# Two diagonal tiles of a head in one bank, masked by a product on the tensor engine

## The reference

```python
q, k, v = jnp.split(jnp.clip(qkv, -8, 8), 3, axis=-1)
q, k = _layer_norm(q, q_ln_w, q_ln_b), _layer_norm(k, k_ln_w, k_ln_b)
...
scores = jnp.einsum('bqhd,bkhd->bhqk', q, k) * HEAD_DIM ** (-0.5)
rel = pos[None, :] - pos[:, None]
bias = slopes[:, None, None] * rel.astype(jnp.float32)
scores = jnp.where(rel <= 0, scores + bias[None], -jnp.inf)
probs = jax.nn.softmax(scores, axis=-1)
attn = jnp.einsum('bhqk,bkhd->bqhd', probs, v)
```

## Time and profile before

| | us |
|---|---|
| median of 3 runs | 1939.48 (1938.72 to 1940.89) |
| the profiled execution | 1937.06 |
| its span, first to last instruction | 1935.3 |
| PE busy | 1842.5 (95%) |
| DVE busy | 1137.5 (59%) |
| POOL busy | 986.4 (51%) |
| ACT busy | 475.4 (25%) |
| pieces on PE, L1823, 384 products | 136.5 |
| masked maxima on DVE, L1698, 256 entries | 115.0 |
| unmasked maxima on DVE, L1702, 128 | 83.2 |

### The profile page before, as it was taken

One profiled execution on the slowest core, in us unless ns is written; L12 is line 12 of the kernel. 1 busy time (PEld: TensorE's weight loads), 2 busy tenths in 40 slices (PEclk: granted clock), 3 DMA queues, 4 the chain that ended last, 5 costly groups with the idle time before them and its releaser, 6 DMA issues. The chain is left out here.

```text
span 1935.3 us, 27511 instructions
## 1 busy us (share of the span) xinstructions
PE 1842.5 (95%) x10157; PEld 1445.1 (75%) x10157; DVE 1137.5 (59%) x1939; ACT 475.4 (25%) x623; POOL 986.4 (51%) x1148
## 2 busy tenths in 40 slices
PE   6999999999999999999999789998889999988998
PEld 5888888888888888888888568886654444357887
DVE  6674674874856747748747733304676888535601
ACT  4221111221211212112112120002414666633200
POOL 5676755755846657557535455444711121235432
PEclk9999999999999999999999899998987999899999
DMA  2111111111111111111101122202043333011112
GB/s 95 46 55 57 45 42 46 43 50 40 43 41 46 49 41 43 39 42 49 49 14 54 44 67 82 68 22 73 3 80 52 56 54 54 2 34 46 48 49 71
DMA packets 50501, 93.57 MB, mean 48 GB/s; under 512 B 8752, under 2 KB 13488, under 8 KB 50032
## 3 DMA queue, kind: packets, MB, share of 16 engines
q1 hardware_dynamic: 49776, 91.13, 17.3%
q10 hardware_dynamic: 640, 1.31, 0.4%
HBM read 76.15 MB, written 2.10 MB: 40 GB/s over the span
## 5 line engine op out<-in xcount | busy, mean ns | idle before, releaser
L366 POOL TENSOR_TENSOR a_w_l<-a_raw,a_w_h 128x1024 fp32r<-128x1024 f32 x96 | 205.6, 2141 | 8.0
L711 DVE TENSOR_TENSOR x<-x,a_ps 128x1024 f32<-128x1024 f32 x64 | 78.0, 1219 | 167.9 <-PE a_ps L165 167.9
L1596 ACT ACTIVATE a_pr<-a_ps 128x1024 f32<-128x1024 f32 (+1 forms) x192 | 153.3, 812 | 90.2 <-PE a_ps L1803 73.2
L1546 POOL TENSOR_SCALAR_AFFINE_SELECT a_pr<-a_pr 128x256 f32<-128x256 f32 x128 | 52.0, 406 | 217.0 <-ACT a_pr L1596 215.3
L1823 PE MATMUL a_ps<-a_K,a_Q 64*128 64x512 f32 (+2 forms) x384 | 136.5, 448 | 11.5 <-DVE a_mx L1702 8.8
L165 PE MATMUL a_ps<-a_tt_h,a_w_l 128*128 128x512 f32 x376 | 147.1, 391 | 0.0
L164 PE MATMUL a_ps<-a_tt_l,a_w_h 128*128 128x512 f32 x376 | 146.6, 390 | 0.0
L163 PE MATMUL a_ps<-a_tt_h,a_w_h 128*128 128x512 f32 x376 | 146.5, 390 | 0.0
L72 POOL TENSOR_TENSOR tick<-neg_half 128x1 f32<-128x1 f32 x120 | 35.0, 292 | 215.2 <-PE a_ps L165 208.1
L1698 DVE CUSTOM_DVE_ANT_0 a_masked<-a_ps,a_mask 128x384 bf16<-128x384 f32 (+3 forms) x256 | 115.0, 486 | 32.5 <-PE a_ps L1823 31.2
L1823 PEld LDWEIGHTS a_ps<-a_K,a_Q 64*128 64x128 f32 x384 | 66.7, 198 | 84.7 <-DVE a_mx L1702 33.4
(11 more groups left out here) (247 smaller groups left out, 4727.7 us busy)
## 6 DMA issues: line engine op xcount, KB each, us to landing
a_raw<-in_a_wpair SPq DMA_DIRECT2D x96, 256.0 KB, 2.7
f_raw<-in_f_w SPq DMA_DIRECT2D x33, 320.0 KB, 2.9
a_raw_s<-in_a_wout SPq DMA_DIRECT2D x32, 256.0 KB, 3.2
f_raw<-in_f_w SPq DMA_DIRECT2D x32, 256.0 KB, 2.6
a_raw_s<-in_a_wv SPq DMA_DIRECT2D x28, 256.0 KB, 2.6
a_cst<-in_a_cst SPq DMA_DIRECT2D x32, 129.0 KB
a_Q<-a_q_h SPq DMA_DIRECT2D x64, 64.0 KB
a_K<-a_k_h SPq DMA_DIRECT2D x54, 64.0 KB
```

What stands on the lines that cost most here:

```text
L366: nc.gpsimd.tensor_tensor(to_l, src, to_h, ALU.subtract).then_inc(s(done), 1)
L711: nc.vector.tensor_tensor(a, a, units[i], ALU.add).then_inc(s("out_added"), 1)
L1546: nc.gpsimd.affine_select(tri, tri, [[0, 2], [1, P]], ALU.is_ge, 0.0, base=0, channel_multiplier=-1).then_inc(s("selected"), 1)
L1596: nc.scalar.activation(pr[n % SLOTS][:, 2 * i:2 * i + 2, 0:width], S[at % 2][:, :, skip:skip + width], ACT.Exp, scale=0.25).then_inc(s("sc ...
```

## The change

The pieces of width 128 of tiles 0 and 4, and those of width 256 of tiles 1 and 5, are made as one item: two score products of 256 columns into the two halves of a bank, each followed by a product `laterb` x `identb` that adds a large negative number above the diagonal of its last 128 columns. One TENSOR_REDUCE takes both maxima. A pair has 20 items and not 24. `AHEAD` and the two bounds around outputs and rows are moved to the same places in the new list, `V_AT` spreads the eight parts over 20 pieces, `paced` counts both tiles of an item, and ACT makes `identb` and `laterb` before it issues its loads.

```diff
--- before.py
+++ after.py
@@ -1290,13 +1290,13 @@
 STEPS += [(kt, max(BANK, kt * P), T - max(BANK, kt * P)) for kt in range(NT)]
 NS = len(STEPS)
 
-PIECES = [(4, 0, BANK, False), (0, 0, P, True), (5, 0, BANK, False), (4, 1, P, True),
-          (6, 0, BANK, False), (1, 0, 2 * P, True), (7, 0, BANK, False), (5, 1, 2 * P, True),
-          (3, 0, BANK, True), (2, 0, 3 * P, True), (7, 1, BANK, True), (6, 1, 3 * P, True)]
+PIECES = [(((4, 0),), BANK, False), (((0, 0), (4, 1)), P, True), (((5, 0),), BANK, False),
+          (((6, 0),), BANK, False), (((1, 0), (5, 1)), 2 * P, True), (((7, 0),), BANK, False),
+          (((3, 0),), BANK, True), (((2, 0),), 3 * P, True), (((7, 1),), BANK, True), (((6, 1),), 3 * P, True)]
 PIECES = [(h, *piece) for piece in PIECES for h in range(2)]
 NP = len(PIECES)
-AHEAD = 8
-V_AT = {2 + 3 * i: (AFTER + i // KT, i % KT) for i in range(2 * KT)}
+AHEAD, MIDDLE, BEHIND = 6, 12, 6
+V_AT = {2 + 5 * i // 2: (AFTER + i // KT, i % KT) for i in range(2 * KT)}
 
 
 def units(m):
@@ -1324,16 +1324,16 @@
     pieces(2, 2, AHEAD)
     for g in range(QUADS):
         p, q = 2 * g + 2, 2 * g + 3
-        pieces(p, AHEAD, 16)
+        pieces(p, AHEAD, MIDDLE)
         if g:
             count("out", g - 1, 1)
-        pieces(p, 16, NP)
+        pieces(p, MIDDLE, NP)
         pieces(q, 0, 2)
         if p < PAIRS:
             count("row", p)
-        pieces(q, 2, 8)
+        pieces(q, 2, BEHIND)
         count("out", g, 0)
-        pieces(q, 8, NP)
+        pieces(q, BEHIND, NP)
         pieces(q + 1, 0, 2)
         if q < PAIRS:
             count("row", q)
@@ -1352,7 +1352,7 @@
     items = list(MAX_AT)
     first = MAX_AT[(2 * g + 2, AHEAD)]
     last = MAX_AT[(2 * g + 4, AHEAD)] if g < QUADS - 2 else MAX_AT[("row", 2 * g + 3)] + 1
-    worth = [PIECES[i[1]][3] + 70 if isinstance(i[0], int) else 350 for i in items[first:last]]
+    worth = [len(PIECES[i[1]][1]) * PIECES[i[1]][2] + 70 if isinstance(i[0], int) else 350 for i in items[first:last]]
     length = sum(2 * n + 100 for _, _, n in STEPS) * 2
     upto, now = [], 0
     for _, _, n in STEPS:
@@ -1611,12 +1611,12 @@
                     act.wait_ge(qs("sh"), m + 1)
                     nc.scalar.activation(cl[:, r, :], cl[:, r, :], ACT.Identity, bias=sh[:, r:r + 1],
                                          scale=rs[:, r:r + 1]).then_inc(qs("normed"), 1)
+            nc.scalar.copy(identb[:, :], ident[:, :]).then_inc(s("later_ready"), 1)
+            act.wait_ge(s("later_in"), 16)
+            nc.scalar.copy(laterb[:, :], later[:, :]).then_inc(s("later_ready"), 1)
             stack(act, 0, 0, (1,))
             stack(act, 1, 0)
             stack(act, 2, 0)
-            nc.scalar.copy(identb[:, :], ident[:, :]).then_inc(s("later_ready"), 1)
-            act.wait_ge(s("later_in"), 16)
-            nc.scalar.copy(laterb[:, :], later[:, :]).then_inc(s("later_ready"), 1)
             act.wait_ge(qs("proj_done"), 3 * NT)
             act.wait_ge(qs("turned_lo"), 16)
             for g in range(QUADS):
@@ -1687,14 +1687,19 @@
             def maximum(p, k):
 
                 at = MAX_AT[(p, k)]
-                h, t, c, width, diagonal = PIECES[k]
+                h, tiles, width, diagonal = PIECES[k]
                 dve.wait_ge(s("max_made"), at + 1)
                 if k == 0 and p >= 2:
                     dve.wait_ge(s("combined"), p - 1)
                 if k == 0 and p == 0:
                     dve.wait_ge(s("mask_in"), 16)
-                to = mx2[p % 2][:, h, t, c:c + 1]
-                if diagonal:
+                first, last = [2 * t + c for t, c in (tiles[0], tiles[-1])]
+                to = mx2[p % 2][:, h, :, :].rearrange("p t c -> p (t c)")[:, first:last + 1:max(last - first, 1)]
+                if len(tiles) == 2:
+                    blocks = M[at % 3].rearrange("p (i q) -> p i q", i=2)
+                    nc.vector.tensor_reduce(to, blocks[:, :, 0:width], AX.X, ALU.max, negate=True
+                                            ).then_inc(s("max_taken"), 1)
+                elif diagonal:
                     nc.vector.tensor_tensor_reduce(
                         out=masked[:, at % 3, 0:width], in0=M[at % 3][:, 0:width], in1=mask[:, BANK - width:],
                         scale=-1.0, scalar=BIG, op0=ALU.add, op1=ALU.min, accum_out=to).then_inc(s("max_taken"), 1)
@@ -1817,12 +1822,19 @@
                 if k == 0:
                     pe.wait_ge(s(f"stack_in{p % SETS}"), stacked(p))
                 out = max_bank(at)
-                h, t, c, width, _ = PIECES[k]
+                h, tiles, width, _ = PIECES[k]
                 rows = slice(ROWS * h, ROWS * (h + 1))
                 w = max(width, 2 * P)
-                nc.tensor.matmul(out[:, 0:w], QT[p % SETS][rows, t * P:(t + 1) * P],
-                                 KTs[p % SETS][rows, c * BANK:c * BANK + w], start=True, stop=True
-                                 ).then_inc(s("max_made"), 1)
+                for i, (t, c) in enumerate(tiles):
+                    last = nc.tensor.matmul(out[:, i * w:(i + 1) * w], QT[p % SETS][rows, t * P:(t + 1) * P],
+                                            KTs[p % SETS][rows, c * BANK:c * BANK + w], start=True,
+                                            stop=len(tiles) == 1)
+                    if len(tiles) == 2:
+                        if (p, k, i) == (0, 2, 0):
+                            pe.wait_ge(s("later_ready"), 2)
+                        last = nc.tensor.matmul(out[:, i * w + width - P:i * w + width], laterb[:, :], identb[:, :],
+                                                start=False, stop=True)
+                last.then_inc(s("max_made"), 1)
 
             def max_row(p):
 
@@ -1873,16 +1885,16 @@
             def maxima(g):
 
                 p, q = 2 * g + 2, 2 * g + 3
-                yield from pieces(p, AHEAD, 16)
+                yield from pieces(p, AHEAD, MIDDLE)
                 if g:
                     yield output(g - 1, 1)
-                yield from pieces(p, 16, NP)
+                yield from pieces(p, MIDDLE, NP)
                 yield from pieces(q, 0, 2)
                 if p < PAIRS:
                     yield max_row(p)
-                yield from pieces(q, 2, 8)
+                yield from pieces(q, 2, BEHIND)
                 yield output(g, 0)
-                yield from pieces(q, 8, NP)
+                yield from pieces(q, BEHIND, NP)
                 yield from pieces(q + 1, 0, 2)
                 if q < PAIRS:
                     yield max_row(q)
```

## The result

| | before | changed |
|---|---|---|
| median | 1940.18 us of 4 runs (1938.72 to 1942.49) | 1972.62 us of 4 runs (1970.66 to 1985.77) |
| the profiled execution | 1937.06 us | 1970.66 us |
| its span | 1935.3 us | 1968.9 us |

The account below looks back on a forecast made before the run. PE and DVE, coupled by three banks, were both near the bound, PE having less idle. Five quads 15.0, seventh 2.2, first 5.9 and prologue 4.0 made 27.1 us, added to the median 1939.48: 1966 us, range 1948 to 1990.

Parts of the forecast that it names:

- DVE's side: One reduce for two masked maxima saves DVE 0.08 us an item, start to start; bounds 0.31 saved and 0.
- PE's item: Product, mask, product, mask take PE 0.94 us alone on the array; less 0.20 for the products before, net 0.74.
- How much is covered: Waits for banks cover half of 5.9 us extra PE work: +3.0 us a quad, 15.0 for five; bounds +1.0, +5.9.
- The first quad: First quad, partly at 1.2 GHz: four items there cost 4.4 us, the other four 1.5, together +5.9 us.
- The prologue: Pieces before any score, mostly at 1.2 GHz: DVE runs dry at merged items, +4.0 us (bounds +1 and +7).
- The seventh quad: Last quad with maxima, six merged items instead of eight: +2.2 us.
- rival 3: Quads and prologue: nothing covered, or clock falls within a quad, 8 to 10 us each; 1990 us, chance 0.15.
- Rival 1: Four places of a quad: masks hidden behind running products, DVE's gain stands; 1934 us, chance 0.08.
- Rival 2: Prologue: more products keep the clock from falling at 1434, 8 us back; 1958 us, chance 0.12.
- Rival 5: Whole kernel: a draw, Rival 1 in half, within 4 us of before; chance 0.04.
- Rival 4: Quads: waits melt as far as they can, only +1.0 us a quad; 1951 us, chance 0.15.
- the signs that were to show the forecast right: PE busy at least 96%, quads 33 to 35 us, piece waits under 4, DVE about 24.5, masks 0.3 behind, first quad near 50.

Follow-up runs that it names:

- masks_last: The change with both score products of an item first, then both masks, in one accumulation group: 1942.26 us, ratio 1.0007.
- two_reduces: masks_64, but DVE takes the two maxima of an item with one reduce each instead of one for both: 1934.22 us, ratio 0.9983.
- order_only: The kernel before with its tiles in the change's order, each in its own bank and masked by DVE: 1940.84 us, ratio 1.0003.
- after_again: The changed kernel run once more, unaltered, for a second trace and more times: 1979.45 us, ratio 1.0201.
- bank_only: The change without its mask products: two tiles share a bank, DVE masks and reduces each half by itself: 1924.91 us, ratio 0.9917.
- masks_twice: The change with each mask product made two times in a row: 1971.07 us, ratio 1.0153.
- masks_64: The change with each mask as two products of 64 rows and 64 columns in the item's own row group, one accumulation group an item: 1934.5 us.
- heads_joint: The change with both heads' items made together in two banks, four score products and then four full-array masks: 1950.81 us, ratio 1.0075.
- bank_128: bank_only with only the 128-column tiles two to a bank, the 256-column tiles in a bank each: 1931.94 us, ratio 0.9949.

## Why the prediction was right, step by step

**What bounds the kernel.** The prediction had PE and DVE coupled by three banks, neither wholly the bound, PE the nearer. Right: packing alone, with DVE's operations the same, took 1.46 us off a quad, and what masks_last took off an item (0.30 us) came off the quad (0.29).

**DVE's side.** 0.08 us an item, start to start, was forecast; two_reduces shows no gain in the quad, and DVE's busy time fell by 0.04 an item. The bound of nothing was nearest to what the runs show. The text's "DVE busy about 24.5 us a quad" contradicted its own term (26.1 less 8 x 0.08 is 25.5) and was wrong: 25.8.

**PE's item.** 0.94 us forecast, 0.94 measured, in its parts 0.31 and 0.16 too. Two rows with pairs of products were enough to build an item that no row showed.

**How much is covered.** +3.0 us a quad forecast, +2.7 measured, but of two terms whose sizes were off, so that the sum came out near is partly luck. The prediction had 5.9 us of PE work, half of it in place of waits for banks; PE's busy time rose by 3.9 us and 1.2 of that filled idle time. The item's 0.94 us was right, so the two products before it took 0.23 us each and not 0.10, if all of the difference is put down to them; in order_only one stands alone for 0.32 us. Measured apart, the mask products cost 4.6 us a quad, and the waits that went are owed to order and packing (0.45 and 1.46 us), which would have been gained without any mask on PE. The place-by-place sum came near because it counted the products at each place with no wait among them. At the two places that the steps of scores part cleanly the measured growth is +0.59 (from 1539.88 to 1543.36 against 2.89 us; forecast +0.6) and +0.98 (from 1568.24 to 1571.83 against 2.61; forecast +0.9).

**The first quad and the prologue.** The first quad was forecast at +5.9 and took +7.5, or +6.3 in after_again, where no second fall begins in it. The stretch at half clock that reaches into it was longer too: 47.8 us in both traces, against 41.0; at the rate above the 6.8 us more cost nearly 3, an estimate. The prologue was forecast at +4.0 and took +2.7. Here too packing hides in it: bank_only's prologue has 29.3 us, so the masks come to 5.5 there; not all of it is their work, for 17.3 us of the change's prologue lie at half clock and 10.2 of bank_only's. The seventh quad was forecast at +2.2 and took +0.5: order_only has 28.8 us there and bank_only 26.9, so order and packing take 2.8 off the 29.7 of before, and the masks put 3.3 on.

**The clock.** The prediction held falls inside a quad in rival 3, at 8 to 10 us each; measured are 1.5 to 6.6 us for a quad, 10.3 and 17.8 us in all. The forecast's own sum was 27.1; without falls the two executions show 21 and 24 (1958.4 and 1960.8 less 1937.06). So the terms overshot by 3 to 6 us in all, and the falls, which the sum left out, added over 10: the step that failed is that they were taken for a rival and not for a term. The two misses have opposite signs, and that 1966 lies within 7 us of 1972.6 owes something to luck.

**The rivals.** Rival 1 (masks hidden) is out by the item's 0.94 us. Rival 2 (the clock stays up in the prologue) is out: it fell at 1433.1. Rival 3 is half right, as said; that the clock falls because the array stands between products is not shown. Rival 5 (a draw) is out by the total. Rival 4's melting waits did take place, some 1.9 us a quad by order and packing, but the masks' price stood on top. Of the signs that were to show the forecast right, the busy share (99.5%), the length of the quads, the 0.31 us ahead of a mask and a first quad near 50 us came; the waits of piece loads did not fall under 4 us (5.5), and DVE's busy time did not fall to 24.5.

**What beats both kernels.** bank_only, the change's order and packing with DVE's masks kept: 1924.91 us, 0.8% under the kernel before.

## What to carry to other kernels

A full-array product among 64-row products cost mostly its change of rows here, 0.29 us a change and back against 0.055 us for a second mask behind the first; so put all products of one kind together, or keep them in the row group of their neighbours, and measure how many banks that asks for at once. Before a bundle of edits is judged, run each part alone: this one held a gain of 15 us (order and packing) under a loss of 48 (masks, with the falls of the clock). Fewer operations on DVE, which waits for PE, were worth nothing here.

## What the runs showed of the hardware that was not expected

The granted clock fell to its lower level (1.2 GHz, 0.5 in the records) within quads in which PE was busy over 99% of the time (97.7% in order_only), and did so at different places in two executions of the same kernel: 13.7 us at 1498.0 and 17.1 us at 1655.0 in one, five falls 34 to 41 us apart in the other. They come in the traces of the change and masks_twice, once in order_only, and in none of the quads with maxima of masks_last, masks_64, two_reduces, heads_joint, bank_only or bank_128 behind the first; in the kernel before only the last 0.8 us of the seventh quad lie in one. How busy PE is does not part them: the steady quads of masks_last and masks_64 are busy 99.4% and stayed at full clock. What brings a fall on stays open: the mask products between score products go with the most of them, but order_only has no such product added and lost 5.1 us in one quad. No run was made to part this further.
